# Dense feed-forward of a gated cross-attention stack: rows normalised by ScalarE, transposes between the two products, context statistics in the first mixture

## The reference

```python
x = x + tanh(g_xattn[1]) * L1_xattn(layernorm(x), ctx_1024, ...)
x = x + tanh(g_ffn[1]) * L1_ffn(layernorm(x), ...)
x = x + tanh(g_xattn[2]) * L2_xattn(layernorm(x), ctx_1024, ctx_1024, ...)
```

```python
h = relu(tgt @ w1[0] + b1[0])
z = tgt + (h @ w2[0] + b2[0])
out = (z - mean(z)) * rsqrt(var(z) + 1e-5) * gamma + beta
```

## Time and profile before

| | before |
|---|---|
| median of 3 runs | 1644.13 us (1643.41 to 1644.64) |
| profiled execution, own time | 1646.58 us |
| its span | 1644.8 us |
| TensorE busy | 1391.0 us (85%) |
| VectorE busy | 1037.0 us (63%) |
| ScalarE busy | 716.7 us (44%) |
| GpSimd busy | 768.4 us (47%) |
| mean granted clock of TensorE | 0.931 |

### The profile page before, as it was taken

How to read it: one execution, slowest core, us unless ns; L and a number is a source line. 1 busy time by engine, 2 the same in 40 slices (tenths; PEclk the granted TensorE clock), 3 DMA queues, 4 the chain that set the end, 5 groups by cost and what they waited for, 6 DMA issues and landing times. The chain is left out here.

```text
span 1644.8 us, 34070 instructions
## 1 busy us (share of the span) xinstructions
PE 1391.0 (85%) x10919; PEld 1114.0 (68%) x10919; DVE 1037.0 (63%) x2336; ACT 716.7 (44%) x1767; POOL 768.4 (47%) x989
## 2 busy tenths in 40 slices
PE   4998776989675877999978986999999999687996
PEld 3777556989565555666645546778788787486984
DVE  4887862414387787999958883545565754363555
ACT  2677453323365324565634442544545445221121
POOL 2554581444371444455434442445444676206445
PEclk9999997999856896999979997999999999898998
DMA  7400123758110000000000000000000000375952
GB/s 187 185 1 2 30 88 108 224 174 265 48 42 2 1 1 1 1 0 0 1 1 0 0 0 1 1 0 0 1 1 1 11 17 19 98 218 174 292 154 83
DMA packets 96485, 100.02 MB, mean 61 GB/s; under 512 B 12149, under 2 KB 69677, under 8 KB 95726
## 3 DMA queue, kind: packets, MB, share of 16 engines
q1 hardware_dynamic: 62322, 69.60, 14.0%
q0 software_dynamic: 8192, 16.79, 3.4%
q10 hardware_dynamic: 25852, 12.09, 2.6%
HBM read 72.23 MB, written 26.21 MB: 60 GB/s over the span
## 5 line engine op out<-in xcount | busy, mean ns | idle before, releaser
L445 POOL TENSOR_TENSOR exp_scores<-exp_scores,softmax_recip 128x308 f32<-128x308 f32 x256 | 181.8, 741 | 181.1 <-DVE softmax_recip L614 180.9
L640 PE MATMUL psum<-identity,exp_scores 128*77 128x128 f32 x1024 | 163.6, 286 | 34.2 <-POOL exp_scores L445 21.6
L1966 POOL TENSOR_TENSOR exp_scores_xattn<-exp_scores_xattn,softmax_recip_xattn 128x1640 f32<-128x1640 f32 x32 | 93.5, 2921 | 162.5 <-DVE softmax_recip_xattn L2139 162.5
L1211 PE MATMUL psum<-sorted_transposed_ffn,tile_weights_up_ffn 128*128 128x128 f32 x1280 | 164.2, 283 | 5.0 <-DVE sorted_transposed_ffn L1099 4.7
L1211 PEld LDWEIGHTS psum<-sorted_transposed_ffn,tile_weights_up_ffn 128*128 128x128 f32 x1280 | 153.8, 197 | 11.7 <-DVE sorted_transposed_ffn L1099 11.5
L640 PEld LDWEIGHTS psum<-identity,exp_scores 128*77 128x77 f32 x1024 | 122.5, 152 | 56.7 <-issue 26.3
L985 POOL DMA_INDIRECT gathered_rows_ffn<-sorted_y,slot_ffn x96 | 90.7, 945 | 104.3 <-DMA sorted_y<-expert_rows_ffn 45.7
L460 ACT COPY probs_transposed<-psum 77x512 f32<-77x512 f32 x192 | 111.1, 581 | 52.2 <-PE psum L640 50.6
L1221 PE MATMUL psum<-expert_weights_down_ffn,hidden_ffn 128*128 x960 | 124.4, 281 | 3.4 <-issue 2.8
L974 POOL DMA_INDIRECT sorted_x<-xn_ffn,slot_ffn x64 | 61.3, 958 | 132.3 <-DVE slot_ffn L859 113.4
L1221 PEld LDWEIGHTS psum<-expert_weights_down_ffn,hidden_ffn 128*128 128x128 f32 x960 | 116.6, 196 | 5.8 <-issue 5.8
(11 more groups left out here) (367 smaller groups left out, 3353.4 us busy)
## 6 DMA issues: line engine op xcount, KB each, us to landing
tile_weights_up_ffn<-in_L_ffn_packed_dram SPq DMA_DIRECT2D x160, 256.0 KB, 3.2
sorted_rows_ffn<-sorted_x SPq DMA_DIRECT2D x80, 128.0 KB, 3.5
sorted_y<-expert_rows_ffn ACTq DMA_DIRECT2D x80, 128.0 KB
sorted_x<-zeros SPq DMA_DIRECT2D x4, 1280.0 KB, 13.4
x_residual<-in_x_dram SPq DMA_DIRECT2D x4, 512.0 KB, 11.1
expert_weights_down_ffn<-in_L_ffn_packed_dram SPq DMA_DIRECT2D x8, 256.0 KB, 15.5
sorted_x<-xn_ffn,slot_ffn POOLq DMA_INDIRECT x128, 2.3
gathered_rows_ffn<-sorted_y,slot_ffn POOLq DMA_INDIRECT x128, 2.7
```

Of the source, the lines that this page charges most:

```text
L445: nc.gpsimd.tensor_tensor(e[:, par, heads, :], e[:, par, heads, :], rec.to_broadcast([S, HG, KC]), ALU.mult).then_inc(s["probs_ready"], 1)
L640: last = nc.tensor.transpose(m.psum[0:KC, 4 + g % 2, h * S:(h + 1) * S], e[:, nxt, g * HG + h, :], m.ident[:, :])
L1211: mm = nc.tensor.matmul(m.psum[:, 2 * (n % 2) + half, to:to + SUB], w[:, n % DEPTH, u, at:at + 128], xst[:, n % 2, u * SUB:(u + 1) * SUB], ...
L1966: nc.gpsimd.tensor_tensor(ev, ev, recip[:, par, :].unsqueeze(2).to_broadcast([S, H3, KV]), ALU.mult).then_inc(s["probs_ready"], 1)
```

## The change

In the dense feed-forward, ScalarE makes the normalised rows of the front part, at the head of its step, with the same two waits that VectorE had; it waits once for the shift of the first normalisation. TensorE does the transposes of group g+1 between up of g and down of g-1. VectorE no longer takes context statistics there: in the first mixture one such instruction follows each of the last 32 tiles.

```diff
@@ sparse_experts, VectorE, per tile n @@
                     route_last(n)
+                    if layer == 0 and n >= NTILES - B:
+                        nc.vector.bn_stats(m.c_moments[:, n - (NTILES - B), :], m.ctx[:, n - (NTILES - B), :])
@@ dense_feed_forward, ScalarE @@
                 act.wait_ge(m.later_loaded, m.later_count)
+                act.wait_ge(s["shift_ready"], 1)
 
                 def step(g, par, front, middle, back, tail):
                     nxt = 1 - par
+                    if front:
+                        wait(act, s["xt_in_psum"], g)
+                        wait(act, s["base_ready"], g)
+                        for t in range(GB):
+                            at = (g + 1) * GB + t
+                            ins = nc.scalar.activation(xn[:, nxt, t, :], m.x[:, at, :], ACT.Identity, scale=m.rstd[:, bass.ds(at, 1)],
+                                                       bias=m.shift[:, bass.ds(at, 1)])
+                        ins.then_inc(s["xn_ready"], 1)
                     if middle:
@@ dense_feed_forward, VectorE @@
-                    if front:
-                        wait(dve, s["xt_in_psum"], g)
-                        wait(dve, s["base_ready"], g)
-                        for t in range(GB):
-                            at = (g + 1) * GB + t
-                            ins = nc.vector.tensor_scalar(xn[:, nxt, t, :], m.x[:, at, :], m.rstd[:, bass.ds(at, 1)],
-                                                          m.shift[:, bass.ds(at, 1)], ALU.mult, ALU.add)
-                        ins.then_inc(s["xn_ready"], 1)
                     if back:
...
-                    if middle:
-
-                        for t in range(GB):
-                            nc.vector.bn_stats(m.c_moments[:, g * GB + t, :], m.ctx[:, g * GB + t, :])
                     if tail:
@@ dense_feed_forward, TensorE @@
                                 .then_inc(s["hidden_in_psum"], 1)
+                    if front:
+                        wait(pe, s["xn_ready"], g + 2)
+                        wait(pe, s["xt_ready"], g + 1)
+                        for t in range(GB):
+                            mm = nc.tensor.transpose(m.psum[:, 5, t * S:(t + 1) * S], xn[:, nxt, t, :], m.ident[:, :])
+                        mm.then_inc(s["xt_in_psum"], 1)
                     if back:
...
                         mm.then_inc(s["y_done"], 1)
-                    if front:
-                        wait(pe, s["xn_ready"], g + 2)
-                        wait(pe, s["xt_ready"], g + 1)
-                        for t in range(GB):
-                            mm = nc.tensor.transpose(m.psum[:, 5, t * S:(t + 1) * S], xn[:, nxt, t, :], m.ident[:, :])
-                        mm.then_inc(s["xt_in_psum"], 1)
```

## The result

| | before | after |
|---|---|---|
| median | 1644.13 us (1643.41 to 1646.65, 5 runs) | 1653.78 us (1651.90 to 1655.18, 5 runs) |
| ratio to before | | 1.0055 (95%: 1.0041 to 1.0069) |
| profiled execution, own time and span | 1646.58, 1644.8 us | 1655.18, 1653.4 us |
| dense feed-forward, first instruction to that of attention 2 | 87.5 us | 93.4 us |
| VectorE busy, whole span | 1037.0 us | 1020.7 us |

The change made the kernel slower, by 0.55%. The forecast was 1650.8 us in a range of 1646.2 to 1655.6.

A forecast was written before the change was run, and what follows sets the result against it. VectorE was taken to set the dense feed-forward's 9.09 us turn before the change. Added waiting of 2.5 us plus clock falls of 4.2 us gave 6.7 us, added to the 1644.13 us median: 1650.8 us, range 1646.2 to 1655.6.

The forecast's parts named there:

- The loop: Dense feed-forward: down, z, square root, ScalarE's rows, transposes, next down wait in a circle; 9.87 us a turn against 9.09.
- The phase without falls: Dense feed-forward at steady clock: start, five turns and end together add 2.5 us.
- z of the first group later: Start of dense phase: slower ScalarE rows (0.37 us) and transposes ahead of down (0.45 us) delay z by 0.82 us.
- five turns at 9.93: Dense phase, z of group 0 to 5: five turns forecast at 49.35 us instead of 45.22, +4.13 us.
- z of group 5 to 6: End of dense phase: no rows left, TensorE runs up and down without a stop; 7.11 us against 8.77, -1.66.
- z of group 6 to 7: End of dense phase: VectorE's queue decides, without four context statistics; 5.04 us against 5.83, -0.79.
- The clock: TensorE pauses of about 2.2 us before five transpose groups let its clock fall in 2.5 of them, +4.2 us.
- rivals B: TensorE's clock falls in every dense-phase pause: 11.0 us slower, 1655.1 us; chance 0.13.
- C: Dense phase turns lengthen as forecast but TensorE's clock holds: 2.5 us slower, 1646.6 us; chance 0.16.
- The statistics cost nothing in the mixture: First mixture: moved context statistics fit VectorE's idle time, cost 0, 0.4 us to spare; not hidden has chance 0.04.
- Rival E: Dense phase: VectorE's collision with GpSimd on small additions goes, turns of 8.92 us, 1641.9 us; chance 0.04.
- Rival D: Dense phase: rows are ready early, no closed circle, TensorE bounds at 7.56 us a turn, 1634.8 us; chance 0.06.

The follow-up runs named there:

- transposes_last: Changed kernel with TensorE's transposes of group g+1 put back behind down of g-1; 1642.98 us, ratio 0.9985 to before.
- rows_ahead: Changed kernel with ScalarE making the rows one group earlier, ahead of the square root of g-1; 1634.95 us, ratio 0.9943 to before.
- transposes_only: Kernel before with only the transposes moved between up and down, rows and context statistics staying on VectorE; 1677.54 us, ratio 1.0192.
- filled_late: Changed kernel with 18 unread identity transposes between up and the transposes, except in the step where TensorE has no pause; 1649.81 us, ratio 1.0021 to before.
- filled: Changed kernel with 18 unread identity transposes between up and the transposes in every step with front and back parts; 1647.51 us, ratio 1.0013 to before.

## Why the prediction was right

**The loop was right, piece by piece.** Forecast 3.77 + 3.76 + 0.21 + 1.63 + 0.05 + 0.45 = 9.87 us; measured 9.93, the 0.06 in the transposes ahead of down (0.49) and the pieces beside them. `transposes_last` opens the loop by TensorE's order, `rows_ahead` by the place of ScalarE's rows, and both remove it: 8.38 and 7.45 us a turn. That this loop needs both, transposes ahead of down and rows behind the square root, is shown. What the prediction did not say is that transposes ahead of down close a longer loop through VectorE where the rows stay there (`transposes_only`, 13.5 us): the rows on ScalarE are not what harms. Its remark that "every engine does the same or less" is wrong for ScalarE, whose busy time from 532 to 622 us rose from 26.8 to 39.2 us; that did not matter, as ScalarE still idles 5.33 us a turn ahead of the square root.

**The phase without falls** came out at 2.6 us for the 2.5 forecast, with small errors that cancel:

| term, us | forecast | measured |
|---|---|---|
| z of the first group later | +0.82 | +0.52 |
| five turns at 9.93 | +4.13 | +4.43 |
| z of group 5 to 6 (7.00 for 8.77) | -1.66 | -1.77 |
| z of group 6 to 7 (5.05 for 5.83) | -0.79 | -0.78 |
| behind it | 0 | +0.24 |

The first is smaller because up of the first group came out of half clock sooner (5.40 us instead of 5.92; over the four profiles the term is 0.5 to 0.8), the last is more because a small addition of four columns now falls beside GpSimd's last sum (0.40 us instead of 0.17, at 622.62). In `filled_late`, where nothing falls, the phase is 3.0 us over before.

**The clock was right in kind, and its size was near with some luck.** Forecast 2.5 falls of 1.7 us, measured 2 of 1.6: 3.3 us for 4.2. That the falls depend on the pause is shown by `filled` and `filled_late`. That they would be about half was taken from two rows, and one of them is weak: the four transposes after the pause of 2.34 us did run at full clock, but TensorE then stood idle for another 3.09 us, and the clock fell in that (0.86 from 177 to 178 us, 0.50 from there):

```profile
175.35 0.63 PE L640 MATMUL psum<-identity,exp_scores 128*77 128x128 f32 x4 [2.34 <-POOL exp_scores L445]
179.07 1.21 PE L711 MATMUL psum<-negated_max,identity_bf 128*128 128x308 bf16 x4 [3.09 <-DVE negated_max L548]
```

The trace of before has five pauses of 2.0 to 2.8 us that began at full clock: after 2.03 and 2.65 us it fell at once, after 2.34 in the next pause, and after 2.04 and 2.71 (ahead of 9.02 and 19.09) it held. That is again two of five, but in other phases with other work; it bounds nothing.

By the traces rivals B (a fall in each pause) and C (none) fell; by the median alone B, at 1655.1, would have been nearer to 1653.78 than the forecast was. The section of the Trainium skill that was weighed, "A second HAM failure mode: psum-queue depth-cycling" of "TensorE: Matmul & The Clock Gate", describes swings from short idle times between groups of matmuls and gives no share of the pauses. Swings are what came: in two of five pauses of 2.3 us, and in five of five of 5.6 to 5.8 us in `transposes_only`.

**The statistics cost nothing in the mixture**, as forecast: 3.79 us a tile, 0.42 us of idle time left for 0.4 forecast.

**Rival E fell**: the small addition still takes 1.12 us (579.75). **Rival D** did not come with this change, but `rows_ahead` is what it described: 7.45 us a turn for 7.56, and 1634.95 us for its 1634.8. (D's sum takes five turns of 9.09 us as the time before, where the other sums take the measured 45.22; by that it is 1635.1.)

**The sum** was 6.7 us; the profiled phase gives 5.9 to 6.1 in all four profiles, of which 2 x 1.6 are falls, while the ratios of 1.0055 and 1.0054 stand for 9 us. So some 3 us of the median are in no term of the forecast, and its being in range owes something to the width of the range. The six profiles do not show them either: without the dense phase the spans are 1557.3 and 1561.1 us before and 1556.3 to 1560.6 after. In them single phases differ between executions of one kernel by up to 2 us (mixture 0: 182.1 and 183.7 before, 181.6 to 183.5 after), and the rest as a whole by 4. Whether the change shifts other phases on average, or the clock falls more often in executions that were not profiled, the runs do not settle.

## What to carry to other kernels

A group of instructions that waits for nothing becomes late when it is put in a queue behind one that waits: follow each moved instruction once round all queues and add the pieces of the closed path, before comparing busy times. Here VectorE got less work, TensorE the same, ScalarE more but far from full, and each turn grew by 0.8 us; the same edits with the rows issued one group earlier were 0.57% faster than before instead of 0.55% slower. And a new pause of TensorE can have a second price, its clock: here about as much again as the loop.

For an effect of a few microseconds in 1650, compare the phase in the profiles before the medians: phases that nobody touched moved by up to 4 us here between kernels.

## What the hardware showed beyond expectation

Useless matmuls paid: 18 transposes into a spare bank in each pause (`filled_late`) took the phase from 93.4 to 90.5 us and the ratio to before from 1.0054 to 1.0021, with the granted clock at 1.00 in all turns. VectorE's gain from dropping 0.78 us of work shrank to 0.25 us because its next instructions moved onto a second GpSimd operation (rows 2.60 instead of 2.08 us). The falls came in the first and in the fourth or fifth of five nearly equal pauses (2.26 to 2.34 us) in all four profiles; what picks them is open.
